# Sums of exponentials placed right behind the products with the values, and VectorE's division ahead of the norm tail, in a fused decoder layer on one Trainium2 core

## The reference, cut to what matters

```python
q = proj(hs, Wq, bq, S); k = proj(at, Wk, bk, T); v = proj(at, Wv, bv, T)
scores = jnp.clip(jnp.einsum('bhsd,bhtd->bhst', q, k) / math.sqrt(HD), -50.0, 50.0)
scores = jnp.clip(jnp.where(attend, scores, -10000.0), -50.0, 50.0)
probs = jax.nn.softmax(scores, axis=-1)
ctx = jnp.einsum('bhst,bhtd->bhsd', probs, v).transpose(0, 2, 1, 3).reshape(B, S, H)
delta = rs * (ctx @ Wo.T + bo)
delta = (delta - mu) / jnp.sqrt(var + EPS_LN) * ln_gamma + ln_beta      # mu, var over the width
x = layernorm(x + delta)
```

## Time and profile before

| what | value |
|---|---|
| median of 3 runs | 1606.23 us (1600.45 to 1606.64) |
| profiled execution: its own time | 1606.45 us |
| profiled execution: span of the trace | 1604.4 us |
| TensorE matmul busy | 1491.7 us, 93% of the span |
| VectorE, ScalarE, GpSimd busy | 1036.6, 643.3, 531.3 us |
| mean granted TensorE clock | 0.969 of full speed |

### The profile page before, as it was taken

How to read it: one execution, slowest core, us unless ns; L and a number is a source line. 1 busy time by engine, 2 the same in 40 slices (tenths; PEclk the granted TensorE clock), 3 DMA queues, 4 the chain that set the end, 5 groups by cost and what they waited for, 6 DMA issues and landing times. The chain is left out here.

```text
span 1604.4 us, 33621 instructions
## 1 busy us (share of the span) xinstructions
PE 1491.7 (93%) x13352; PEld 1150.3 (72%) x13352; DVE 1036.6 (65%) x2051; ACT 643.3 (40%) x834; POOL 531.3 (33%) x488
## 2 busy tenths in 40 slices
PE   7999999996999999999999999999999963998994
PEld 3688888875887877788787887878788742554652
DVE  2766666644266767677666766767676673775797
ACT  2233333331333333333333333334333321989761
POOL 0000000000144444443444444444443443651552
PEclk9999999998899999999999999999999976999997
DMA  6022222223212121211212111121211103276953
GB/s 203 27 82 86 95 95 95 96 99 114 75 43 64 36 73 36 69 40 39 70 36 73 36 54 55 36 73 36 73 36 43 48 14 86 70 275 258 360 159 93
DMA packets 61748, 138.53 MB, mean 86 GB/s; under 512 B 4674, under 2 KB 29762, under 8 KB 59906
## 3 DMA queue, kind: packets, MB, share of 16 engines
q1 hardware_dynamic: 61698, 137.84, 26.4%
HBM read 93.78 MB, written 44.04 MB: 86 GB/s over the span
## 5 line engine op out<-in xcount | busy, mean ns | idle before, releaser
L700 POOL TENSOR_TENSOR xa_psum<-xa_pr 125x448 f32<-125x448 f32 x128 | 147.2, 1150 | 464.9 <-DVE xa_pr L840 464.9
L873 PE MATMUL xa_bKV<-xa_cx,wA 128*128 128x376 f32 x1536 | 289.5, 338 | 7.4 <-DVE xa_cx L766 7.4
L886 PE MATMUL xa_bKV<-wZ,xa_cx 128*125 128x512 f32 x1152 | 289.2, 399 | 0.0
L873 PEld LDWEIGHTS xa_bKV<-xa_cx,wA 128*128 128x128 f32 x1536 | 266.7, 189 | 21.9 <-issue 13.1
L886 PEld LDWEIGHTS xa_bKV<-wZ,xa_cx 128*125 128x125 f32 x1152 | 208.7, 186 | 55.1 <-issue 10.6
L786 DVE RECIPROCAL xa_rinv<-xa_bPV 128x112 f32<-128x112 f32 x128 | 109.5, 855 | 160.8 <-PE xa_bPV L927 160.8
L750 ACT ACTIVATE xa_pr<-xa_bSC 125x1344 f32<-125x1344 f32 x128 | 165.5, 1293 | 74.4 <-PE xa_bSC L941 74.4
L729 ACT ACTIVATE xa_kf<-xa_bKV,xa_bk 128x376 f32<-128x376 f32 x128 | 73.6, 575 | 297.7 <-PE xa_bKV L873 297.6
L840 DVE TENSOR_SCALAR xa_pr<-xa_pr,xa_keep 125x448 f32<-125x448 f32 x384 | 151.5, 451 | 43.7 <-ACT xa_pr L750 43.7
L703 POOL TENSOR_TENSOR xa_psum<-xa_psum,xa_pr 125x448 f32<-125x448 f32 x128 | 157.1, 1227 | 12.3 <-POOL xa_psum L700 4.4
L735 ACT COPY xa_v<-xa_bKV 125x512 f32<-125x512 f32 x96 | 56.4, 588 | 203.8 <-PE xa_bKV L886 203.8
(11 more groups left out here) (167 smaller groups left out, 2164.1 us busy)
## 6 DMA issues: line engine op xcount, KB each, us to landing
wraw<-in_ctxT SPq DMA_DIRECT2D x32, 752.0 KB, 5.6
ff_hr<-h_scratch SPq DMA_DIRECT2D x4, 3584.0 KB, 15.2
wraw<-in_w SPq DMA_DIRECT2D x8, 1024.0 KB, 7.6
sa_raw<-in_x SPq DMA_DIRECT2D x8, 896.0 KB, 5.9
x_scratch<-sa_qraw SPq DMA_DIRECT2D x8, 896.0 KB, 5.1
xa_qf<-q_scratch SPq DMA_DIRECT2D x32, 224.0 KB, 5.5
xa_x<-x_scratch SPq DMA_DIRECT2D x32, 224.0 KB, 5.0
x_scratch<-xa_x SPq DMA_DIRECT2D x32, 224.0 KB, 2.3
```

The lines of the kernel that those rows point to most:

```text
L700: nc.gpsimd.tensor_tensor(psum01[:], third(h, 0), third(h, 1), ALU.add).then_inc(p01_ok, 1)
L873: mm = nc.tensor.matmul(bKV[par][:, 0:TP], w["k"][l][:, c, m * P:(m + 1) * P], cx[par][r][:, c, :], start=c == 0 and k == 0, stop=c == C - ...
L886: mm = nc.tensor.matmul(bKV[1 - par][0:TW, 0:D], cx[par][l][:, c, t * TW:(t + 1) * TW], w["v"][r][:, c, :], start=c == 0 and k == 0, stop= ...
```

## The change

On TensorE, `sums` is called directly behind `attend` in each slot, ahead of `output`, `values` and `keys`. On VectorE, `attended` is called directly behind the three clamps, ahead of `tail1` and `tail2`. No instruction is added or removed, and no semaphore count changes.

```diff
 # VectorE, body of cross_attention
                     for t in range(TC):
                         ...
                         nc.vector.tensor_scalar(third(h, t), third(h, t), EM50, bound, ALU.max, ALU.min).then_inc(pr_ok, 1)
+                    if h > 0:
+                        attended(b, h - 1)
+                    elif not first(b):
+                        attended(b - 1, C - 1)
                     if not first(b):
                         if h == 1:
                             tail1(b - 1, 1 - par)
                         if h == 2:
                             tail2(b - 1, 1 - par)
-                    if h > 0:
-                        attended(b, h - 1)
-                    elif not first(b):
-                        attended(b - 1, C - 1)
                     if h == 3 and not first(b):
                         tail3(b - 1, 1 - par)
 # TensorE, body of cross_attention
                     if h > 0:
                         attend(b, par, h - 1)
+                        sums(b, h - 1)
                     elif not first(b):
                         attend(b - 1, 1 - par, C - 1)
+                        sums(b - 1, C - 1)
                     if h == 1 and not first(b):
                         output(b - 1, 1 - par)
                     if not last(b):
                         ...
                         keys(b + 1, 1 - par, h)
                         if h == 0:
                             values(b + 1, 1 - par, 0)
-                    if h > 0:
-                        sums(b, h - 1)
-                    elif not first(b):
-                        sums(b - 1, C - 1)
```

## The result

The changed kernel takes 1567.82 us in the median (1565.43 to 1569.06), the kernel before 1605.7 us in the runs beside it. The ratio is 0.9764, with a 95% interval of 0.975 to 0.9778. Forecast were 1571.6 us in a range of 1562 to 1588, and faster with a chance of 0.94.

The account below looks back on a forecast made before the run. TensorE, covered 98.55% by matmuls, was taken to bound the cross-attention, so only time lost between matmuls could be won. 16.8 + 16.0 + 1.8 = 34.6 us off 1606.45 gives 1571.9, in the median 1571.6; range 1562 to 1588.

Parts of the forecast that it names:

- The wait for `cT`: Slot 1, batches 1 to 30: the output product's 0.56 us wait for the divided rows goes, 16.8 us won.
- The check beside it: TensorE's waits for the divided rows: the waits view, without its longest, gives 16.1 us over 31, agreeing with 16.8.
- The order on TensorE: Sums right behind the products in 123 slots: 0.13 us saved each, 16.0 us, bounds 0 and 24.6.
- Rival B: TensorE's products and sums: the gap only moves and the pair saves nothing, 1587.6 us; chance 0.10.
- The cover: Slot 0: GpSimd's add of group 3 ends 0.54 us before its earlier sums start, so it costs nothing.
- Rival A: Slot 0: GpSimd's adds of group 3 come too late and TensorE waits, 1572 to 1586 us; chance 0.12.
- Rival C: Slot 0: the wait for the adds outgrows a batch's 1.08 us gain, making it slower, 1626 us; chance 0.06.
- VectorE and GpSimd side by side: L794 grows by 0.79 us beside GpSimd's adds, L816 shrinks by 0.93; slot 2's VectorE chain stays within 0.2.
- `tail1` behind `attended`: Slots 1 to 2: the bank is free at 8.0 us, before values at 8.55, so it costs nothing.
- The end: Last batch: attended runs while VectorE waits for the output product, 1.8 us won, bounds 0 and 3.5.

Follow-up runs that it names:

- the run with the sums amid the keys: Changed kernel with sums put between the two full-width products of each slot, not behind the products with the values: 1611.28 us, ratio 1.003.
- the two runs that used it up: Changed kernel with one or two more VectorE instructions of L807's shape behind tail2 in slot 2: 1570.97 us (0.9794) and 1592.22 us (0.9925).
- The run with slot 0 alone: Against the kernel before, sums moved behind the products in slot 0 only, VectorE in its old order: 1584.07 us, ratio 0.9873.
- TensorE's half alone: Changed kernel with VectorE back in its old order, sums still right behind the products: 1566.88 us, ratio 0.9775.
- the changed kernel again: Changed kernel repeated without edits, on the chip of the two versions beside it: 1568.01 us, ratio 0.9779.
- the run with VectorE's half alone: Against the kernel before, attended moved ahead of the tails on VectorE, sums left at the slot's end: 1655.17 us, ratio 1.0322.

## Why the prediction was right, point by point

- **The wait for `cT`.** 16.8 us forecast. It is gone in batches 1 to 30, with 3 us to spare rather than 1.5: in slot 0 GpSimd's second add comes too late to hold L794 (0.8 us), and the clamps of slot 0 start 2.57 us into the slot instead of 3.17 (0.6 us). Right. The check beside it was not: the 16.1 us over 31 waits count the 1.73 us before the output of batch 30, which stands in the last batch and stayed as a wait of 1.59 us at the sums. The other 30 waits come to 14.4 us by the waits view, which counts from the modelled end of the products; the starts give 16.8.
- **The order on TensorE.** 0.13 us a slot forecast from the pair of the earlier trace rows, 0.11 to 0.16 measured (slot 1 after its 0.56 of wait). That 0.13 came from the pair itself and not from the bounds is what made it good. Both terms together were 32.8 us in the forecast (16.8 + 16.0), and 32.8 were measured between the first scores and the last batch. Rival B is out: its gap did go, and the run with the sums amid the keys shows that it follows the steps from shape to shape, not the wait.
- **The cover.** 0.54 us forecast, 0.58 measured, and shown by the two runs that used it up. Rival A did not come, and its mechanism is the wrong way round: `split_low` starts 0.13 us ahead of L693, and L693 is held (2.00 us instead of 0.55) where nobody waits for it. Rival C stays a matter of more than one such instruction; two extra ones, 1.4 us, gave 24 of the 38 us back and did not turn the sign.
- **VectorE and GpSimd side by side.** L816 went from 1.68 to 0.75 as forecast. The hold was given to L794 in every slot; in fact it is L794 in slots 2 and 3, L792 in slot 1, and in slot 0 the add (1.30) instead. None of it reached TensorE.
- **`tail1` behind `attended`.** Nothing forecast, nothing measured: in slot 1 the bank is free 6.99 us after the slot's start and `values` want it at 8.55. One wait on this path was not in my account. L792 of slot 1 writes the tile that the output product reads and waited for it, 0.36 us in the row above; there was room for it.
- **The end.** 1.8 us forecast, 2.3 measured, and that it came near is luck: the step is wrong in its reason. I gave it to `attended` running while VectorE waits. With VectorE's old order the last batch is as short (39.67 against 39.48). Most of it is TensorE's clock, as the two stretches of the output product of batch 30 show, before the change and after it:

```profile
1301.10:1306.60 5.50, 5.49 (x16) 3.58 (x20) 2.07 (x3) 0.00 (x0) 3.36 (x3) 0.50 0.08 28
```
```profile
1266.30:1270.00 3.70, 3.64 (x32) 2.53 (x36) 3.46 (x7) 0.00 (x0) 2.56 (x4) 1.00 0.00 0
```

Before, TensorE waited 1.73 us ahead of that product and then ran it at half the clock, 5.46 us. After, it waited 1.59 us, ahead of the sums, and the product took 3.03 us at full clock. Of those 2.4 us nothing was in my sum. It would be easy to read from these two rows that the shorter idle kept the clock. Two experiments of the record speak against it. The same 1.73 us of waiting, in the run with the sums amid the keys, was followed by full clock, 3.03 us. The same 1.59 us, in the run with one extra VectorE instruction (L930 and L902 are L927 and L899), was followed by a product of 4.60 us:

```profile
1307.37 3.03 PE L899 MATMUL xa_bKV<-wQ,xa_cT 128*112 128x512 f32 x12 [1.73 <-DVE xa_cT L794]
```
```profile
1264.99 0.40 PE L930 MATMUL xa_bPV<-xa_psum,xa_ones 125*32 125x112 f32 x8 [1.59 <-POOL xa_psum L704]
1265.32 4.60 PE L902 MATMUL xa_bKV<-wQ,xa_cT 128*112 128x512 f32 x12
```

What the order gives in the last batch can be read without the clock. Take the two output products in it out of its length: before 41.82 - 5.46 - 4.33 = 32.03 us, after 39.48 - 3.03 - 4.96 = 31.49. The run with slot 0 alone, whose last batch has the order of the kernel before, gives 32.03 too; TensorE's half alone and the changed kernel again give 31.49 and 31.47. By this count the order is worth 0.54 us there, and 1.80 of the 2.34 come from the products' clock. Why the clock fell in some executions and not in others stays open.

- **The remainder.** 1571.6 against 1567.8, 3.8 us: about 0.5 us is the end, 2.2 us lie outside the cross-attention's loop and last batch, and 1.0 is that the median now lies 1.2 us below the profiled execution instead of the 0.2 I took over. Neither of the last two is the change's: the same kernel, profiled again, has a span of 1563.9 us instead of 1567.0, with the same 838.42 us of loop.

## What to carry to other kernels

Where one engine is 98% busy and in order, read the distance between starts instead of durations: it shows what each neighbour costs, and the ends of a loop (first and last turn) can already show, as here, an order that the middle doesn't have. Put work of the same tiling shape side by side, and put the producer of a value that others wait for at the first place where its inputs are there, after counting how much cover those inputs have. A division or a tail moved ahead on a waiting engine is only as good as the release it waits for: alone, the same move on VectorE cost 51 us here. And where a loop repeats to a hundredth of a microsecond, read a change of a few us from the loop of the trace: the parts around it vary by more between executions of kernels that are the same there.

## What the runs showed of the hardware that was not expected

- In the last batch the granted clock of a nearly idle TensorE falls to 0.50 and the output product then takes 5.46 us instead of 3.03; with matmuls that compute nothing useful in the idle time it was 1.00 and the last batch 2.4 us shorter. The product before it, of batch 30, took from 3.03 to 5.46 us in the traces, and the length of the wait ahead of it does not tell which.
- A VectorE instruction with one SBUF tensor (L792, 0.28 us alone) is held by GpSimd's adds as one with two is: 1.10 us in slot 1, and 0.84 beside L685 in the run with VectorE's half alone. The Trainium skill, "SBUF — State Buffer", in "Who interferes with whom", on the shared port pair, gives the hold to perf modes and to two SBUF inputs; this instruction has one, so by that page it would have to be in such a mode, which no run here shows.
- On this evidence the hold goes by which of the two starts first, both ways: L693 waits behind L766 (2.00 us instead of 0.55), and L703 behind L794 by 0.16 us (1.30).
